# One semaphore for each step of a recurrence, attention with a row to a token, and an up projection parted by columns, in a four-layer conditioned stack on one core

## The chip, the cores and the metric

The kernel runs on one core of a Trainium2 chip. The metric is the device time of one execution in microseconds (us), smaller is better. Three executions of the kernel before took 1957.75, 1958.13 and 1960.11 us; their median is 1958.13.

## What is computed

The input x has 2 sequences of 1024 tokens of width 256, the condition one vector of 256 for each sequence. Four layers follow, each added to x, all in float32:

```python
x = x + L0(x, cond)   # 16 heads over two keys: a learned one and one from cond
x = x + L1(x, cond)   # shared SwiGLU expert (512) + top-2 of 8 gelu experts (128), sum / 3
x = x + L2(cond, x)   # gelu(cond @ Wp + bp) @ Wu + x @ We
x = x + L3(x, cond)   # the recurrence:
#   z = x_t @ Wx + b + h @ Wh;  i, f, o = sigmoid of three quarters, g = tanh of the fourth
#   c = f * c + i * g;  h = o * tanh(c);  the output is h of each of the 1024 tokens
```

Layers 0 to 2 work on each token alone. Layer 3 is serial: step t needs the h of step t-1, 1024 steps in all, for two sequences side by side.

## The kernel before, in words

**One loop, 8 steps to a batch.** The tokens are taken in 128 batches of U = 8 steps (NB = 16 rows: 8 steps by 2 sequences). Each engine has its own loop over the batches; TensorE, ScalarE and VectorE unroll the 8 steps, u = 0 to 7. Layers 0 to 2 of the coming batches are parted into fillers that are placed between the pieces of the recurrence. READY = 16 is the value at which the loops' semaphores start.

**A step of the recurrence.** TensorE waits on `hid`, one semaphore that VectorE raises by 1 at each step; the value it waits for is made by `pe.snap(t + (u + 1))` in every step. Then come `recur_row` for f and for i (L943: 8 products each, h as the weights of a 32 column group of the array, 64 columns moving) and `recur_column` for g and o (L953: 16 products each, 2 columns moving). A float32 product is two weight loads and two matmul records here, so L943 shows 32 of each kind in a step and L953 64. VectorE transposes f and i (L744, L746), ScalarE takes tanh of f (L526), of i and g (L529), of o (L532) and of the cell (L535); VectorE multiplies (L753), forms the cell by a scan (L756), and `close` (L703) writes the new h into `h_ring` and raises `hid`. GpSimd reads h_ring once in a batch, behind the same semaphore.

**TensorE's fillers** stand behind L953 of each step, in program order:

- u = 0: `stream_mm` (L829, 4 products of 128 columns) and `down_mm(0)` (L836, 4 of 256)
- u = 1: `scores` (L793) and `route` (L805, L807) for the next batch, into PSUM bank 5
- u = 2: `down_mm(1)`
- u = 3: `down_mm(2)`, then `attend` (L798): 4 products, value_w as weights of 64 columns, `w1_own` (16 columns) moving; its output `attn_b` has the channels on the partitions. It waits for `mask` of VectorE (L583). All other fillers but the last two products of `route` use column groups of 32
- u = 4: `sum_mm` (L843) and `up_mm` (L815) for K half 1 of the shared expert, 4 products of 256 columns
- u = 5: `up_mm` for K half 0 of all units, 4 products of 512 columns
- u = 6: `inject` (L855), 8 products of 256 columns
- u = 7: `up_mm` for K half 1 of the routed experts, 4 products of 256 columns

The up projection has its sums in `units`, PSUM bank 5, 512 columns: shared expert 0 to 255, the two routed experts of each group 256 to 383 and 384 to 511.

**VectorE's own extras.** At u = 1, behind `close`, `attended` (L599) adds attn_b (PSUM) and x_a (SBUF) into x1, the weights of the next products; it waits for `stream_made` of u = 0. Transposes of the hidden units (L612) are at u = 1, 2 and 7, layer 3's input (L615) and the bias copy (L622) at u = 5; nothing stands at the head of u = 6. VectorE runs in program order, so what stands between `close` and L744 can delay L744.

**ScalarE's extras.** Router and score tanh (L479, L541) at u = 1, `take_partial` (L496) at u = 3, which waits until `attend` is done, the shared tanh (L483) at u = 5 and the gelu (L487) at u = 7.

**GpSimd** runs some 30 small operations for the top-2 gates of a batch, in one chain from L392 to L382, waiting for three reciprocals of VectorE; then `weigh` (L444, which also needs the gelu), the output of the batch (L464, L469) and `move` (L449, a copy of x3 from SBUF to SBUF).

**Before the loop** the weights are loaded and folded and two batches go through layers 0 to 2, with the same helpers; `attend` runs twice there, `attended` twice.

Of the kernel before, what the change touches and what calls it, by code (L numbers as in the profile page):

```python
# [6 lines left out]
ALU = mybir.AluOpType  # L7
# [4 lines left out]
P = 128  # L12
B, T, D = 2, 1024, 256
C = D // P
# [9 lines left out]
U = 8  # L24
# [38 lines left out]
def cond_stack_kernel(nc, x, small, wkv, wq, wproj, up, we, down, wproj2, wu, wx, wh, bias_z, y):  # L63
    ctx = ExitStack()
    with ctx:
# [66 lines left out]
        w1 = sb("w1", [B * HEADS, NB])  # L132
        w1_own = sb("w1_own", [P, NB])
        x1 = sb("x1", [P, C, J, 32])
# [77 lines left out]
        x3_b = bank[7][:, D:D + C * NB].rearrange("p (c t) -> p c t", c=C)  # L212
        attn_b = bank[7][:, D + C * NB:D + 2 * C * NB].rearrange("p (c t) -> p c t", c=C)

        scores_first_b = bank[6][0:B * HEADS, 64:64 + LEAD * NB]
        attn_first_b = bank[6][:, 128:128 + 2 * C * NB].rearrange("p (c n t) -> p c n t", c=C, n=2)
        route_t_b = bank[7][0:B, 448:448 + E]
# [36 lines left out]
        own_out = sem("own_out")  # L254
        attn_made = sem("attn_made")
        x1_out = sem("x1_out")
        route_made = sem("route_made")
# [44 lines left out]
        cell_tanh = sem("cell_tanh")  # L302
        hid = sem("hid")
        h_read = sem("h_read")
# [46 lines left out]
        def _(pool):  # L351
            pool.sem_inc(y_stored, 16)
            for s in (f_made, i_made, o_made, f_turned, a_f, cell, cell_tanh, hid, x_turned, i_based):
                pool.sem_inc(s, READY)
# [104 lines left out]
            with pool.Fori(0, BATCHES) as i:  # L459
                gates(i * U + (READY + U), fall[:, :])  # L460
                weigh(i * U + (READY + U)).then_inc(hid_e_out, U)

                pool.wait_ge(hid, i * U + (READY + U + 1))
                pool.tensor_tensor(half_h[:].rearrange("p c (u b) -> p u c b", b=B), h_ring[:, :, :, WIN - B:WIN],  # L464
                                   half[:, :].unsqueeze(2).unsqueeze(3).to_broadcast([P, U, C, B]),
                                   ALU.mult).then_inc(h_read, U)
                pool.wait_ge(h_read, i * U + (READY + 2 * U))
                pool.wait_ge(y_stored, i * 16 + 16)
                pool.tensor_tensor(y_sb[:, :, :], x3[:, :, 0:NB], half_h[:, :, :], ALU.add).then_inc(y_made, U)  # L469
                pool.wait_ge(y_made, i * U + U)  # L470
                move().then_inc(moved, U)
# [77 lines left out]
        def _(dve):  # L549
# [32 lines left out]
            def mask(src, done, up_to):  # L582
                nc.vector.scalar_tensor_tensor(out=w1_own[0:B * HEADS, :], in0=src, scalar=1.0, in1=own,  # L583
                                               op0=ALU.add, op1=ALU.mult).then_inc(done, up_to)
# [13 lines left out]
            def attended(dst, attn, src):  # L598
                nc.vector.tensor_tensor(dst[:, :, :, 0:NB], attn.unsqueeze(2).to_broadcast([P, C, J, NB]),  # L599
                                        src.unsqueeze(2).to_broadcast([P, C, J, NB]), ALU.add).then_inc(x1_out, U)  # L600

            def hidden_a(count):
# [42 lines left out]
            dve.wait_ge(attn_made, 1)  # L645
            attended(x1_first, attn_first_b[:, :, 0, :], x_first[:, 0, :, :])
            attended(x1, attn_first_b[:, :, 1, :], x_first[:, 1, :, :])
            invert_ratio(U)
# [48 lines left out]
            dve.wait_ge(x_injected, READY)  # L697
            base_f(READY + U)
            dve.wait_ge(terms_set, 5)

            def close(slot):

                nc.vector.scalar_tensor_tensor(out=h_ring[:, slot, :, WIN - B:WIN],  # L703
                                               in0=o_act[:, :].rearrange("p (c b) -> p c b", b=B), scalar=1.0,
                                               in1=c_tanh.rearrange("p (c b) -> p c b", b=B),
                                               op0=ALU.add, op1=ALU.mult).then_inc(hid, 1)


            with dve.Fori(READY, READY + T, U) as t:
                now = t  # L710
                for u in range(U):
# [11 lines left out]
                    elif u == 1:  # L723
                        dve.wait_ge(x_ready, now)
                        dve.wait_ge(stream_made, now)
                        attended(x1, attn_b, x_a[:, :, :])
                    elif u == 2:
                        turn(2, hid_e[:, P:2 * P], hid_e1t, U)
                    elif u == 3:
                        dve.wait_ge(w1_out, now)  # L730
                        mask(w1[:, :], own_out, U)
                    elif u == 4:
                        invert_s(now)
                    elif u == 5:
                        dve.wait_ge(x3_made, now)
                        dve.wait_ge(moved, now)
                        layer3(U)
                    elif u == 7:
                        hidden_s(now)
                        invert_inv(now)  # L740
                        dve.wait_ge(hid_s_out, now)
                        turn(0, hid_s[:, :], hid_st, U)
# [27 lines left out]
        def _(pe):  # L770
# [20 lines left out]
            def scores():  # L791
                for c in range(C):
                    nc.tensor.matmul(scores_b, score_w[:, c, :], x_s[:, c, :], start=(c == 0), stop=(c == C - 1))  # L793

            def attend(attn, weights):
                for c in range(C):
                    for j in range(0, P, 64):
                        last = nc.tensor.matmul(attn[j:j + 64, c], value_w[:, c * P + j:c * P + j + 64], weights,  # L798
                                                start=True, stop=True, skip_group_check=True)
                return last  # L800
# [9 lines left out]

            SHARED, EXPERTS, ALL = slice(0, 2 * P), slice(2 * P, 4 * P), slice(0, 4 * P)

            def up_mm(c, which, first, src):
# [65 lines left out]
            pe.wait_ge(own_first, 1)  # L879
            attend(attn_first_b, own_both[:, :].rearrange("p (n t) -> p n t", n=2)).then_inc(attn_made, 1)  # L880
            pe.wait_ge(value_out, 3)
# [54 lines left out]
            pe.wait_ge(own_first, 2)  # L936
            attend(attn_b, w1_own[:, :])
            pe.wait_ge(wh_scaled, 2)
# [19 lines left out]

            with nc.Fori(READY, READY + T, U, engines=(PE_ENGINE,), head_slot={PE_ENGINE: 0}) as t:
                for u in range(U):  # L960
                    prev = (u - 1) % U
                    now = pe.snap(t + (u + 1))

                    pe.wait_ge(hid, now)
                    recur_row(z_f, GF, u * B, prev).then_inc(f_made, 1)
# [18 lines left out]
                    elif u == 2:  # L984
                        pe.wait_ge(hid_e0t, now)
                        down_mm(1)
                    elif u == 3:
                        pe.wait_ge(hid_e1t, now)
# [4 lines left out]
                    elif u == 4:  # L993
                        pe.wait_ge(partial_out, now)
                        sum_mm().then_inc(x3_made, U)
                        up_mm(1, SHARED, True, x1)
                    elif u == 5:

                        up_mm(0, ALL, False, x1).then_inc(up_made, U)
                    elif u == 6:  # L1000
# [100 lines left out]
```

## Time and profile before

| what | value |
|---|---|
| median of three executions | 1958.13 us |
| the profiled execution | 1957.56 us |
| its span, first to last instruction | 1955.8 us |
| granted TensorE clock, mean | 0.996 |

The profile counts an engine as busy from the start to the modelled end of each instruction; matmuls are pipelined, so busy intervals of TensorE run over one another and reach past the time at which the array can take the next product. PE is the matmul record, PEld the weight load. A row of the timeline gives start, length, engine, line and operation, and in brackets how long the engine was idle before it and what released it. A row with xN merges N records: its length is that of the whole group. The other 1.8 us (1957.56 less 1955.8) lie outside the span.

### The profile page before, as it was taken

The numbers are of one execution on the slowest core, as the hardware profiler recorded it, in microseconds if no ns is written. First come the engines' busy times: TensorE is split into PE (matmuls) and PEld (weight loads), VectorE is DVE, ScalarE is ACT, GpSimd is POOL, SyncE is SP. The second block draws the span as 40 slices with busy tenths as digits, with TensorE's granted clock in tenths as the row PEclk, the third lists the DMA queues.
The fourth block names the chain that finished last, engine by engine and source line by source line (L and its number), as shares of the span: only waits on it lengthen the run. The fifth ranks groups of instructions, "written<-read, shape, count | busy, mean of one in ns | idle before, by whom it ended". The sixth has DMA issues, their size and how long they took to land.

```text
span 1955.8 us, 256304 instructions
## 1 busy us (share of the span) xinstructions
PE 1889.5 (97%) x113680; PEld 1439.8 (74%) x113680; DVE 1390.7 (71%) x7217; ACT 827.2 (42%) x4757; POOL 1133.8 (58%) x4950
## 2 busy tenths in 40 slices
PE   7999999999999999999999999999999999999998
PEld 5777777777777777777777777777777777777776
DVE  2677777777777777777777777777777777777776
ACT  1344444444444444444444444444444444444444
POOL 4555655655555565565555556555555655665565
PEclk9899999999999999999999999999999999999999
DMA  4000000000000000000000000000000000000000
GB/s 170 4 4 3 3 4 3 3 3 4 3 3 4 3 3 3 4 3 3 4 3 3 4 3 3 3 4 3 3 4 3 3 3 4 3 3 4 3 3 3
DMA packets 57724, 14.67 MB, mean 8 GB/s; under 512 B 56176, under 2 KB 56304, under 8 KB 57200
## 3 DMA queue, kind: packets, MB, share of 16 engines
q1 hardware_dynamic: 57712, 14.50, 3.2%
q8 instruction: 9, 0.15, 0.0%
q14 instruction: 3, 0.02, 0.0%
HBM read 12.37 MB, written 2.10 MB: 7 GB/s over the span
## 4 chain that ended last, share of the span: by engine, by line
PE 87%; ACT 6%; DVE 4%; issue 2%; DMA 0%; POOL 0%; DVEq 0%; SPq 0%; POOLq 0%; ACTq 0%
PE psum L953 29%; PE psum L943 29%; PE psum L815 10%; PE psum L836 7%; PE psum L855 6%; DVE h_ring L703 3%; ACT o_act L532 3%; ACT psum L535 2%; PE psum L798 2%; PE psum L829 2%; PE psum L843 1%; PE psum L892 1%; PE psum L793 0%; DMA wkv_sb<-in_wkv 0%; PE psum L776 0%
## 5 line engine op out<-in xcount | busy, mean ns | idle before, releaser
L943 PEld LDWEIGHTS psum<-wh_sb,h_ring 128*2 128x2 f32 (+1 forms) x32768 | 488.4, 90 | 416.6 <-DVE h_ring L703 409.8
L953 PE MATMUL psum<-h_ring,wh_sb 128*32 128x2 f32 x65536 | 765.7, 173 | 1.8 <-issue 1.8
L953 PEld LDWEIGHTS psum<-h_ring,wh_sb 128*32 128x32 f32 x65536 | 725.8, 109 | 2.0 <-issue 2.0
L943 PE MATMUL psum<-wh_sb,h_ring 128*2 128x64 f32 (+1 forms) x32768 | 656.8, 220 | 50.8 <-DVE h_ring L703 20.2
L526 ACT ACTIVATE f_act<-psum 128x4 f32<-128x4 f32 x1024 | 177.3, 173 | 698.6 <-DVE psum L744 698.6
L744 DVE STREAM_TRANSPOSE psum<-psum 128x64 f32<-128x64 f32 x1024 | 266.1, 260 | 274.6 <-PE psum L943 262.7
L815 PE MATMUL psum<-up_sb,x 128*32 128x256 f32 (+1 forms) x3096 | 311.8, 460 | 0.0
L746 DVE STREAM_TRANSPOSE psum<-psum 128x64 f32<-128x64 f32 x1024 | 271.5, 265 | 1.9 <-PE psum L943 1.9
L703 DVE SCALAR_TENSOR_TENSOR h_ring<-o_act,psum 128x4 f32<-128x4 f32 x1025 | 163.0, 159 | 141.9 <-ACT psum L535 115.9
L836 PE MATMUL psum<-down_e,hid_t 128*16 128x256 f32 x3096 | 251.6, 382 | 0.6 <-ACT down_e L507 0.6
L756 DVE TENSOR_TENSOR_SCAN psum<-addend,psum 128x16 f32<-128x16 f32 x1024 | 199.3, 195 | 52.2 <-ACT psum L529 2.4
L532 ACT ACTIVATE o_act<-psum 128x4 f32<-128x4 f32 x1024 | 177.3, 173 | 128.5 <-PE psum L953 2.1
L529 ACT ACTIVATE psum<-psum 128x8 f32<-128x8 f32 x1024 | 165.9, 162 | 54.7 <-PE psum L953 2.6
L753 DVE SCALAR_TENSOR_TENSOR addend<-f_act,psum 128x4 f32<-128x4 f32 x1024 | 165.9, 162 | 14.3
L535 ACT ACTIVATE psum<-psum 128x4 f32<-128x4 f32 x1024 | 161.8, 158 | 0.0
L392 POOL TENSOR_TENSOR num<-one,fall 128x8 f32<-128x8 f32 x128 | 25.6, 200 | 228.6 <-ACT fall L479 228.6
L855 PE MATMUL psum<-wx_sb,x 128*16 128x256 f32 x2064 | 140.0, 381 | 0.4 <-issue 0.4
L398 POOL TENSOR_TENSOR num<-num 128x8 f32<-128x8 f32 x520 | 103.5, 199 | 40.8
L395 POOL TENSOR_TENSOR num<-num,ratio 128x8 f32<-128x8 f32 x130 | 27.1, 208 | 121.0 <-DVE ratio L588 121.0
L444 POOL TENSOR_TENSOR hid_e<-gelu_act,gate_w 128x256 f32<-128x256 f32 x130 | 79.7, 613 | 26.4 <-ACT gelu_act L487 26.1
L798 PEld LDWEIGHTS psum<-w_own,value_w 128*64 128x64 f32 x1032 | 40.7, 137 | 55.2 <-issue 55.2
L496 ACT ACTIVATE partial<-psum 128x256 f32<-128x256 f32 x129 | 49.6, 384 | 71.1 <-PE psum L798 69.8
(142 smaller groups left out, 2286.0 us busy)
## 6 DMA issues: line engine op xcount, KB each, us to landing
x_a<-in_x SPq DMA_DIRECT2D x129, 16.0 KB, 1.6
x_s<-in_x SPq DMA_DIRECT2D x129, 16.0 KB, 1.6
up_sb<-in_up SPq DMA_DIRECT2D x1, 2048.0 KB, 12.7
out_y<-y_sb SPq DMA_DIRECT2D x128, 16.0 KB, 1.4
down_sb<-in_down SPq DMA_DIRECT2D x1, 1536.0 KB, 8.3
wx_sb<-in_wx SPq DMA_DIRECT2D x1, 1024.0 KB, 14.5
wh_sb<-in_wh SPq DMA_DIRECT2D x1, 1024.0 KB, 16.6
wkv_sb<-in_wkv SPq DMA_DIRECT2D x1, 512.0 KB, 4.4
```

The source lines that it names most:

```text
L526: nc.scalar.activation(f_act[:, :].rearrange("p (c b) -> p c b", b=B), by_row(t_f)[:, :, step], ACT.Tanh).then_inc(a_f, 1)
L532: nc.scalar.activation(o_act[:, :].rearrange("p (c b) -> p c b", b=B), by_row(z_o)[:, :, step], ACT.Tanh)
L535: nc.scalar.activation(c_tanh, cell_c, ACT.Tanh).then_inc(cell_tanh, 1)
L703: nc.vector.scalar_tensor_tensor(out=h_ring[:, slot, :, WIN - B:WIN], in0=o_act[:, :].rearrange("p (c b) -> p c b", b=B), scalar=1.0, in1= ...
L744: nc.vector.transpose(t_f, z_f).then_inc(f_turned, 1)
L746: nc.vector.transpose(t_i, z_i).then_inc(i_and_c_in, 1)
L756: nc.vector.tensor_tensor_scan(cell_all, addend[:, :], factor, 0.0, ALU.add, ALU.mult).then_inc(cell, 1)
L815: last = nc.tensor.matmul(units[32 * j:32 * (j + 1), which], src[:, c, 0, :], up_sb[:, c, j, which], start=first, stop=not first, skip_gro ...
L836: last = nc.tensor.matmul(partial_b[32 * k:32 * k + NB, :], hid_t[:, blk * 32:blk * 32 + NB], down_e[:, blk, :], start=False, stop=False, ...
L855: last = nc.tensor.matmul(z_x[32 * j:32 * j + NB, :, :], x3[:, c, NB:2 * NB], wx_v[:, c, :, j, :], start=False, stop=(c == C - 1), skip_gr ...
L943: last = nc.tensor.matmul(z[32 * j:32 * j + row + B, :], h_ring[:, prev, c, WIN - B - row:WIN], wh_v[:, c, g, j, :], start=False, stop=(c ...
L953: last = nc.tensor.matmul(by_row(z)[32 * j:32 * (j + 1), m, row:row + B], wh_v[:, c, g, j, 32 * m:32 * (m + 1)], h_ring[:, prev, c, WIN - ...
```

## The change

All steps: `hid` becomes a list of 8 semaphores, one for each u, each raised by U = 8 once in a batch; TensorE forms its register `now` once in a batch, not once in a step. `close(slot)` raises `hid[(slot + 1) % U]`.

Attention: `w1_own` becomes 32 columns wide and is the weight operand; 4 products with 64 moving columns of value_w write a row to a token, 32 rows to each of the four groups of partitions. VectorE transposes the 128x64 result in blocks of 32 into `attn_t` in SBUF, at the head of u = 6, behind a wait on `x1_out`; `attended` at u = 1 reads `attn_t`, behind a wait on `attn_turned`. The same goes for the two batches before the loop, whose two attentions become one call of 4 products, one transpose and two `attended`; one more transpose stands ahead of VectorE's loop.

Up projection: the columns of the second routed expert (384 to 511) of K half 0 move from u = 5 to u = 2, behind `down_mm(1)` and a wait on `w1_out`; u = 5 keeps 384 columns.

```diff
-        w1_own = sb("w1_own", [P, NB])
+        w1_own = sb("w1_own", [P, 32])
+        attn_t = sb("attn_t", [P, C, 32])
+        attn_first_t = sb("attn_first_t", [P, C, 32])
...
-        attn_b = bank[7][:, D + C * NB:D + 2 * C * NB].rearrange("p (c t) -> p c t", c=C)
+        attn_b = bank[7][:, D + C * NB:D + C * NB + HC]
...
-        attn_first_b = bank[6][:, 128:128 + 2 * C * NB].rearrange("p (c n t) -> p c n t", c=C, n=2)
+        attn_first_b = bank[6][:, 128:128 + HC]
...
-        hid = sem("hid")
+        hid = [sem(f"hid_{u}") for u in range(U)]
...
-                pool.wait_ge(hid, i * U + (READY + U + 1))
+                pool.wait_ge(hid[0], i * U + (READY + 2 * U))
...
+            def turn_attention(up_to):
+                nc.vector.transpose(attn_t[:, :, :].rearrange("p c t -> p (c t)"), attn_b).then_inc(attn_turned, up_to)
...
-            attended(x1_first, attn_first_b[:, :, 0, :], x_first[:, 0, :, :])
-            attended(x1, attn_first_b[:, :, 1, :], x_first[:, 1, :, :])
+            nc.vector.transpose(attn_first_t[:, :, :].rearrange("p c t -> p (c t)"),
+                                attn_first_b).then_inc(attn_turned, U)
+            dve.wait_ge(attn_turned, U)
+            attended(x1_first, attn_first_t[:, :, 0:NB], x_first[:, 0, :, :])
+            attended(x1, attn_first_t[:, :, NB:2 * NB], x_first[:, 1, :, :])
...
             base_f(READY + U)
+            dve.wait_ge(attn_made, 2)
+            turn_attention(READY)
             dve.wait_ge(terms_set, 5)
...
-                                               op0=ALU.add, op1=ALU.mult).then_inc(hid, 1)
+                                               op0=ALU.add, op1=ALU.mult).then_inc(hid[(slot + 1) % U], U)
...
                         dve.wait_ge(stream_made, now)
-                        attended(x1, attn_b, x_a[:, :, :])
+                        dve.wait_ge(attn_turned, now)
+                        attended(x1, attn_t[:, :, 0:NB], x_a[:, :, :])
...
+                    elif u == 6:
+                        dve.wait_ge(x1_out, now)
+                        turn_attention(U)
...
+            value_v = value_w[:, :].rearrange("p (c j m) -> p c j m", c=C, j=J)
+
             def attend(attn, weights):
-                for c in range(C):
-                    for j in range(0, P, 64):
-                        last = nc.tensor.matmul(attn[j:j + 64, c], value_w[:, c * P + j:c * P + j + 64], weights,
-                                                start=True, stop=True, skip_group_check=True)
+                for j in range(J):
+                    last = nc.tensor.matmul(attn[32 * j:32 * (j + 1), :], weights, value_v[:, :, j, :],
+                                            start=True, stop=True, skip_group_check=True)
                 return last
...
+            BUT_EXPERT_1, EXPERT_1 = slice(0, 3 * P), slice(3 * P, 4 * P)
...
+                now = pe.snap(t + U)
                 for u in range(U):
                     prev = (u - 1) % U
-                    now = pe.snap(t + (u + 1))
-                    pe.wait_ge(hid, now)
+                    pe.wait_ge(hid[u], now)
...
                     elif u == 2:
                         pe.wait_ge(hid_e0t, now)
                         down_mm(1)
+                        pe.wait_ge(w1_out, now)
+                        up_mm(0, EXPERT_1, True, x1)
...
                         sum_mm().then_inc(x3_made, U)
-                        up_mm(1, SHARED, True, x1)
+                        up_mm(1, SHARED, False, x1)
                     elif u == 5:
-                        up_mm(0, ALL, False, x1).then_inc(up_made, U)
+                        up_mm(0, BUT_EXPERT_1, False, x1).then_inc(up_made, U)
```

## Rows read from the trace of the kernel before

**Rows 1.** The page, part 1, then two groups of its part 5 (busy us, mean ns | idle before, releaser)

```profile
PE 1889.5 (97%) x113680; PEld 1439.8 (74%) x113680; DVE 1390.7 (71%) x7217; ACT 827.2 (42%) x4757; POOL 1133.8 (58%) x4950
...
L943 PEld LDWEIGHTS psum<-wh_sb,h_ring 128*2 128x2 f32 (+1 forms) x32768 | 488.4, 90 | 416.6 <-DVE h_ring L703 409.8
...
L798 PEld LDWEIGHTS psum<-w_own,value_w 128*64 128x64 f32 x1032 | 40.7, 137 | 55.2 <-issue 55.2
```

**Rows 2.** The timeline, `close` (L703) on VectorE at ten places: start us, us

```profile
41.92 0.16 DVE L703 SCALAR_TENSOR_TENSOR h_ring<-o_act,psum 128x4 f32<-128x4 f32 x1
...
65.74 0.16 DVE L703 SCALAR_TENSOR_TENSOR h_ring<-o_act,psum 128x4 f32<-128x4 f32 x1 [0.22 <-ACT psum L535]
...
1001.36 0.16 DVE L703 SCALAR_TENSOR_TENSOR h_ring<-o_act,psum 128x4 f32<-128x4 f32 x1 [0.22 <-ACT psum L535]
...
1003.18 0.16 DVE L703 SCALAR_TENSOR_TENSOR h_ring<-o_act,psum 128x4 f32<-128x4 f32 x1 [0.22 <-ACT psum L535]
...
1008.65 0.16 DVE L703 SCALAR_TENSOR_TENSOR h_ring<-o_act,psum 128x4 f32<-128x4 f32 x1 [0.22 <-ACT psum L535]
...
1010.60 0.16 DVE L703 SCALAR_TENSOR_TENSOR h_ring<-o_act,psum 128x4 f32<-128x4 f32 x1 [0.22 <-ACT psum L535]
...
1012.43 0.16 DVE L703 SCALAR_TENSOR_TENSOR h_ring<-o_act,psum 128x4 f32<-128x4 f32 x1
...
1014.32 0.16 DVE L703 SCALAR_TENSOR_TENSOR h_ring<-o_act,psum 128x4 f32<-128x4 f32 x1
...
1016.21 0.16 DVE L703 SCALAR_TENSOR_TENSOR h_ring<-o_act,psum 128x4 f32<-128x4 f32 x1 [0.22 <-ACT psum L535]
...
1951.76 0.16 DVE L703 SCALAR_TENSOR_TENSOR h_ring<-o_act,psum 128x4 f32<-128x4 f32 x1 [0.22 <-ACT psum L535]
```

**Rows 3.** The timeline, step u = 1 of one batch

```profile
1003.39 0.45 PEld L943 LDWEIGHTS psum<-wh_sb,h_ring 128*4 128x4 f32 x32 [0.43 <-DVE h_ring L703]
...
1003.87 0.27 DVE L744 STREAM_TRANSPOSE psum<-psum 128x64 f32<-128x64 f32 x1
...
1005.21 0.45 PEld L943 LDWEIGHTS psum<-wh_sb,h_ring 128*6 128x6 f32 x32 [0.17 <-DVE h_ring L703]
```

**Rows 4.** Stretches: us, busy us (x records) of the five engines, clock, DMA share, GB/s

```profile
50.00:55.00 5.00, 4.34 (x171) 3.38 (x163) 1.56 (x8) 1.13 (x6) 2.33 (x9) 0.50 0.02 3
...
500.00:514.85 14.85, 14.47 (x888) 11.03 (x887) 10.79 (x57) 6.40 (x38) 8.71 (x38) 1.00 0.02 3
```

**Rows 5.** DMA queues from 36 to 66 us: packets, MB, share

```profile
q8 instruction: 8, 0.13, 1.9%
```

**Rows 6.** The timeline, end of step u = 3 of the same batch, TensorE

```profile
1008.07 0.64 PE L836 MATMUL psum<-down_e,hid_t 128*16 128x256 f32 x7
...
1008.64 0.31 PEld L798 LDWEIGHTS psum<-w_own,value_w 128*64 128x64 f32 x8 [0.42 <-issue]
...
1008.98 0.46 PEld L943 LDWEIGHTS psum<-wh_sb,h_ring 128*10 128x10 f32 x32
```

**Rows 7.** The timeline, steps u = 5 and 6 of the same batch, TensorE

```profile
1011.85 1.08 PE L815 MATMUL psum<-up_sb,x 128*32 128x512 f32 x7
...
1012.64 0.55 PEld L943 LDWEIGHTS psum<-wh_sb,h_ring 128*14 128x14 f32 x32 [0.62 <-DVE h_ring L703]
...
1012.71 0.66 PE L943 MATMUL psum<-wh_sb,h_ring 128*14 128x64 f32 x32
```

**Rows 8.** The timeline, before the loop and at its start

```profile
41.51 0.41 PE L798 MATMUL psum<-w_own,value_w 128*64 128x16 f32 x8
```

**Rows 9.** The timeline, step u = 1 of the same batch, GpSimd and VectorE

```profile
1003.50 0.21 POOL L449 COPY x<-x 128x32 f32<-128x32 f32 x1
...
1003.59 0.29 DVE L599 TENSOR_TENSOR x<-psum,x_a 128x128 f32<-128x128 f32 x1 [0.26 <-PE psum L836]
```

**Rows 10.** A line of VectorE with both inputs in SBUF: duration ns min/median/max, first and last start

```profile
L631 DVE TENSOR_TENSOR we_sb<-we_sb,small_sb x2: 270/270/271, 12.8 to 13.0; 128x128 f32<-128x128 f32 x2
```

**Rows 11.** The page, part 5: `weigh` on GpSimd

```profile
L444 POOL TENSOR_TENSOR hid_e<-gelu_act,gate_w 128x256 f32<-128x256 f32 x130 | 79.7, 613 | 26.4 <-ACT gelu_act L487 26.1
```

More of the change, by code:

```diff
@@ L255, in cond_stack_kernel @@
         attn_made = sem("attn_made")
+        attn_turned = sem("attn_turned")
         x1_out = sem("x1_out")
@@ L352, in _ @@
             pool.sem_inc(y_stored, 16)
-            for s in (f_made, i_made, o_made, f_turned, a_f, cell, cell_tanh, hid, x_turned, i_based):
+            for s in (f_made, i_made, o_made, f_turned, a_f, cell, cell_tanh, x_turned, i_based, *hid):
                 pool.sem_inc(s, READY)
@@ L582, in mask @@
             def mask(src, done, up_to):
-                nc.vector.scalar_tensor_tensor(out=w1_own[0:B * HEADS, :], in0=src, scalar=1.0, in1=own,
+                nc.vector.scalar_tensor_tensor(out=w1_own[0:B * HEADS, 0:NB], in0=src, scalar=1.0, in1=own,
                                                op0=ALU.add, op1=ALU.mult).then_inc(done, up_to)
@@ L879, in _ @@
             pe.wait_ge(own_first, 1)
-            attend(attn_first_b, own_both[:, :].rearrange("p (n t) -> p n t", n=2)).then_inc(attn_made, 1)
+            attend(attn_first_b, own_both[:, :]).then_inc(attn_made, 1)
             pe.wait_ge(value_out, 3)
@@ L936, in _ @@
             pe.wait_ge(own_first, 2)
-            attend(attn_b, w1_own[:, :])
+            attend(attn_b, w1_own[:, :]).then_inc(attn_made, 1)
             pe.wait_ge(wh_scaled, 2)
```

## The prediction

> **What bounds the kernel now.** The page comes first, and it misleads: TensorE is busy for 97% of the span [rows 1]. In the same rows its weight loads for the next h (L943) stood idle for 409.8 us until `close` had written h, so TensorE waits for VectorE in most steps. The second view is the timeline, read only for the starts of `close`, which are 1 step apart [rows 2]. One batch takes 1016.21 - 1001.36 = 14.85 us, and all but the first do: (1951.76 - 65.74) / 127 = 14.85. The first takes 65.74 - 41.92 = 23.82. Within the batch the step of u = 0 takes 1.82, those of u = 1, 2 and 3 together 5.47 (1.82 each), u = 4 takes 1.95, u = 5 takes 1.83, and u = 6 and 7 take 1.89 each.
>
> Steps with quite different fillers take the same 1.82 us, so there the serial chain decides. The third view, one such step, shows it [rows 3]: first weight load at 1003.39, transpose of f at 1003.87, the next step's first load at 1005.21, 1.82 later, after TensorE had been idle for 0.17. What the change can win without shortening that chain is what the three long steps have above 1.825: 0.12 at u = 4, 0.065 at u = 6, 0.065 at u = 7, together 0.25 us in a batch, or 32 us over 128. For each of them I ask which filler held TensorE.
>
> *u = 4.* The filler of u = 3 is too long [rows 6]. The eight matmul records of `down_mm(2)` begin at about 1008.06. At the rate worked out below (54 ns for one of 256 columns) the array has taken them by 1008.49, yet the loads of `attend` begin only at 1008.64, and L943 at 1008.98, though h was written at 1008.65 + 0.16 = 1008.81 [rows 2]. From 1008.49 to 1008.98 is 0.49 us for `attend`, with 0.15 empty ahead of it (the trace puts 0.42 us of idle loader time down to "issue", and the page has 55.2 us of that in the whole run, all at this line [rows 1]). It is the only filler here with weights 64 columns wide. I take that the array has to run empty between the two widths, before and after.
>
> *u = 6.* The filler of u = 5 is eight records of 512 columns [rows 7], from 1011.84. The next step's loads start in time, at 1012.64, its matmuls at 1012.71: late by 0.07. So eight records of 512 columns take 12.71 - 11.84 = 0.87 us, 109 ns each, 54 for 256 columns, 27 for 128, 14 for 64.
>
> *u = 7.* `inject` has 16 records of 256 columns, 0.87 us as well, and is not touched.
>
> **The change part by part.**
>
> *Attention in four products.* Four products of 64 columns are eight records, 8 x 14 = 0.11 us, in groups of 32 columns like their neighbours. Then TensorE is through at 1008.49 + 0.11 = 1008.60, 0.21 before h is there, and the step of u = 4 begins with h: it goes from 1.95 to about 1.83. By `close` the gain is 0.12 in a batch. It can't be more, since the chain holds the step then, and the other end is nothing, should the new products wait as long as the old ones. I take 0.12, as the two changes of width are gone. `take_partial` on ScalarE starts earlier by some 0.3 us, which no one waits for.
>
> *The transpose.* VectorE gets one more STREAM_TRANSPOSE of 128x64 at the head of u = 6; its like takes 0.27 [rows 3]. It is put between `close` and L744, a stretch of VectorE from 1003.34 to 1003.87 in a step without extras (0.16 after `close` starts at 1003.18, until f is there [rows 2, 3]), so 0.53 wide. 0.27 fits, with 0.2 or more to spare; price 0. If the cover went, the price would be what reaches past L744. Its wait on `x1_out` is for an operation of VectorE itself, five steps back. `attended` at u = 1 waits on `attn_turned`, three steps old by then; price 0 as well.
>
> *`attended` from SBUF.* Now 0.29 us from PSUM and SBUF, 1003.59 to 1003.88, and L744 starts at 1003.87 [rows 3, 9]: this one has no slack. With both inputs in SBUF an operation of the same size took 0.270 [rows 10]. Price 0, at best 0.02.
>
> *128 columns of the up projection moved.* u = 5 keeps 384 columns: 8 x 82 = 0.66 us, through at 1012.50, ahead of h (1012.43 + 0.16 = 1012.59). So the step of u = 6 loses its 0.065. At u = 2, `down_mm(1)` (0.44) gets 0.22 behind it: 0.66, as much as u = 0 has now with 128 and 256 columns, and the step behind u = 0 is not late: 1003.39 is 0.05 after h (1003.34) [rows 2, 3]. The wait on `w1_out` is for ScalarE's operation behind the step before; u = 0 has a wait between its two fillers too. Behind it in TensorE's queue stands the step of u = 3, so were it late, all would be; I price it at 0. Gain 0.065, bounds 0 and 0.07.
>
> *One semaphore for each step, one register.* The only thing that it removes is TensorE's forming of a register ahead of each wait. In seven steps of eight TensorE idles there anyway, 0.17 us in the fullest of those shown [rows 3]: covered. L943 starts 0.05 after the end of `close` (1003.34 to 1003.39); I can bound a gain by a hop of nothing, 0.05 x 1024 = 51 us, but I see no register in that gap, since it would be formed before h comes. Price 0. Without that cover, it would be one register operation for each step, for which no row has a time.
>
> *Before the loop and its first batch.* The transpose ahead of the first `attended` and the one ahead of the first `close` cost 0.27 each with nothing beside them; `attend` at 41.51, 0.41 long with its last end [rows 8], gives about 0.3 back, but only the second time does VectorE wait near it. Sum +0.5, bounds 0 and +0.7. The first batch takes 8.97 us longer than the others. Instructions come in over their own queue at that time (8 packets, 0.13 MB, from 36 to 66 us [rows 5]) and the granted clock is at 0.50, the 1.2 GHz level, from 50 to 55 us, after TensorE had stood still for want of instructions; later it is at 1.00 [rows 4]. The loop's body has some 1775 records [rows 4] and gets 16 more. How that falls on the packets is not to be read from here: 0, with bounds of -4 and +4.
>
> **The sum.** (0.12 + 0.065) x 127 batches = 23.5 us less, 0.5 more: 1957.56 - 23.0 = 1934.6 for the profiled execution. That execution is 0.57 under the median of three, so against the median it would be 1935.1. I say 1935.
>
> **The rivals.**
>
> *A, the forecast* (0.72): the two long steps become chain-bound. 1935; with the first batch's bounds and 0.03 a batch for a residue or for a little of the 0.02 at `attended`, 1930 to 1941.
>
> *B, half of it* (0.13): one of the two steps stays late. Only the columns: 1958 - 8 = 1950. Only the attention: 1958 - 15 = 1943. For it speaks that the gap ahead of `attend` bears the name "issue" and not that of a width; against it that no other filler shows it.
>
> *C, the chain gets shorter too* (0.06): the register or the value compared lies between h and L943 after all. If it has 0.01 to 0.02 of the 0.05, another 10 to 20 us: 1915 to 1925. Against it: TensorE has been idle for 0.17 to 0.43 us at that point [rows 3].
>
> *D, slower* (0.05): `attended` and GpSimd get into each other's way at u = 1. At present `move` (L449) runs from 1003.50 to 1003.71 and reads SBUF, and `attended` starts at 1003.59 beside it with one input from PSUM [rows 9]. With two inputs from SBUF it may have to wait until L449 is done. L744 follows at once, so each ns of it is in the step. The price is up to 1003.71 - 1003.59 + 0.1 = 0.22 us a batch, 28 us: 1963. It decides from 0.18 us on, where it eats up the 23 us; at 0.1 it leaves 1948. Against it: GpSimd gains only some 0.1 us in the batch that gets shorter by 0.185, since `weigh` waits for the gelu now (26.1 us in 128 batches, 0.20 each [rows 11]) and then for its own gates; so L449 would start about 0.08 later against `attended`, and VectorE may well be first. The Trainium skill, "SBUF — State Buffer", section "Who interferes with whom", states the rule: a VectorE instruction with two SBUF inputs contends with a GpSimd instruction that reads SBUF, and whoever issues first has the port for the whole instruction. No row here shows VectorE with two SBUF inputs beside a busy GpSimd for long enough to tell. By that rule the result depends on who is first.
>
> *E, it doesn't do what it says* (0.04): some wait is late in a way that I don't see, or both steps keep their length: 1957 to 1960.
>
> **How the numbers follow.** About 0.2% (4 us) can be told from no change. Faster by more: A, B and C, 0.72 + 0.13 + 0.06 = 0.91. Within: E, 0.04. Slower: D at more than the 0.18, 0.05. The range is A's own 1930 to 1941, carried up to 1948, so that it takes in the columns failing (1943) and a D at half price. C, D, E and the upper half of B are left out, about 0.2.
>
> **What would show it.** Right: `close` to `close` is 1.82 or 1.83 in all steps but u = 7 (1.89); a batch takes 14.665; no "issue" idle at the line of `attend`; L943's loads follow h by 0.05 at u = 4. The matmuls of u = 6 start with their loads. Wrong: a step of u = 1 above 1.82 with `attended` starting later than 0.25 after `close` has ended is D; all steps below 1.82 is C; an idle loader ahead of `attend` or of the columns at u = 2 is B; a first batch far from 23.8 is the start's bounds.

## The result and the profile after

The changed kernel takes 2007.75 us (median of four, 2006.75 to 2008.01) against 1958.28 for the kernel before; the ratio is 1.025 with a 95% interval of 1.0232 to 1.0268. It is slower by 49 us where the forecast said faster by 23. The profiled execution has 2007.65 us, its span 2005.7, its mean granted clock 0.997 (0.996 before).

From the page of the changed kernel: part 1, the instruction queue, then two groups of part 5 (the loads for the next h, and `close`). The second block is the group of `close` in the kernel before, L703:

```profile
PE 1906.6 (95%) x114704; PEld 1466.1 (73%) x114704; DVE 1436.8 (72%) x7347; ACT 832.3 (41%) x4757; POOL 1141.9 (57%) x4950
...
q8 instruction: 9, 0.15, 0.0%
...
L963 PEld LDWEIGHTS psum<-wh_sb,h_ring 128*2 128x2 f32 (+1 forms) x32768 | 467.8, 90 | 460.6 <-DVE h_ring L716 458.4
...
L716 DVE SCALAR_TENSOR_TENSOR h_ring<-o_act,psum 128x4 f32<-128x4 f32 x1025 | 163.1, 159 | 204.0 <-ACT psum L540 177.0
```

```profile
L703 DVE SCALAR_TENSOR_TENSOR h_ring<-o_act,psum 128x4 f32<-128x4 f32 x1025 | 163.0, 159 | 141.9 <-ACT psum L535 115.9
```

TensorE waits more for h (458.4 us at L963, 409.8 before [rows 1]), and VectorE waits more, in `close`, for ScalarE's tanh of the cell: 177.0 against 115.9 us. Each `close` is as long as before, 159 ns. The chain of the step has become longer, between those two instructions. Lines of one step (u = 3 of one batch) and the start of the next, changed kernel:

```profile
1002.38 0.45 PEld L963 LDWEIGHTS psum<-wh_sb,h_ring 128*8 128x8 f32 x32 [0.28 <-DVE h_ring L716]
...
1002.86 0.27 DVE L761 STREAM_TRANSPOSE psum<-psum 128x64 f32<-128x64 f32 x1 [0.31 <-PE psum L963]
...
1003.58 0.20 DVE L773 TENSOR_TENSOR_SCAN psum<-addend,psum 128x16 f32<-128x16 f32 x1
1003.63 0.38 PEld L817 LDWEIGHTS psum<-value_w,w_own 128*32 128x32 f32 x8
...
1003.81 0.16 ACT L540 ACTIVATE psum<-psum 128x4 f32<-128x4 f32 x1
1003.84 0.32 PE L817 MATMUL psum<-value_w,w_own 128*32 128x64 f32 x8
1004.07 0.16 DVE L716 SCALAR_TENSOR_TENSOR h_ring<-o_act,psum 128x4 f32<-128x4 f32 x1 [0.29 <-ACT psum L540]
...
1004.28 0.46 PEld L963 LDWEIGHTS psum<-wh_sb,h_ring 128*10 128x10 f32 x32 [0.28 <-DVE h_ring L716]
```

The same places in the kernel before:

```profile
1004.58 0.20 DVE L756 TENSOR_TENSOR_SCAN psum<-addend,psum 128x16 f32<-128x16 f32 x1
...
1004.81 0.16 ACT L535 ACTIVATE psum<-psum 128x4 f32<-128x4 f32 x1
1005.00 0.16 DVE L703 SCALAR_TENSOR_TENSOR h_ring<-o_act,psum 128x4 f32<-128x4 f32 x1
```

A step is 1004.28 - 1002.38 = 1.90 long, not 1.82. Load to transpose is 0.48 as in [rows 3], scan to tanh 0.23 in both, `close` to the next load 0.21 in both. From the start of the tanh to that of `close` it is 0.26 here and 0.19 before: 0.07 more, and no other part of the step has changed by more than 0.01. `attend` is where it was forecast: its loads start at 1003.63 with no idle time, and L963 at 1004.28 had waited 0.28 for h.

By the starts of `close`, medians over the 128 batches, in us:

| step u | 0 | 1 | 2 | 3 | 4 | 5 | 6 | 7 | batch | first batch |
|---|---|---|---|---|---|---|---|---|---|---|
| before | 1.82 | 1.82 | 1.83 | 1.83 | 1.94 | 1.83 | 1.89 | 1.88 | 14.85 | 23.82 |
| forecast | 1.82 | 1.82 | 1.83 | 1.83 | 1.83 | 1.83 | 1.83 | 1.89 | 14.67 | 23.8 |
| changed | 1.88 | 1.89 | 1.90 | 1.90 | 1.90 | 1.90 | 1.90 | 1.96 | 15.23 | 25.14 |

The changed kernel is the forecast plus 0.07 in every step: 8 x 0.07 = 0.56 a batch, 71 us over 127 batches, with the 23.5 us of gain inside.

### The profile page after: what moved, and what is told of

Read it like the earlier page. It is cut to its first block, busy times and chain, and to the rows that moved or that the text cites. A ratio compares the mean times of both kernels' runs of the same rounds, so it can differ in the third digit from the quotient of the medians.

```text
span 2005.7 us, 258620 instructions
## 1 busy us (share of the span) xinstructions
PE 1906.6 (95%) x114704; PEld 1466.1 (73%) x114704; DVE 1436.8 (72%) x7347; ACT 832.3 (41%) x4757; POOL 1141.9 (57%) x4950
## 2 busy tenths in 40 slices
DMA packets 57724, 14.67 MB, mean 7 GB/s; under 512 B 56176, under 2 KB 56304, under 8 KB 57200
## 4 chain that ended last, share of the span: by engine, by line
PE 82%; ACT 8%; DVE 5%; issue 4%; DVEq 1%; POOL 0%; DMA 0%; SPq 0%; POOLq 0%; ACTq 0%
PE psum L963 30%; PE psum L973 29%; PE psum L835 7%; PE psum L856 6%; PE psum L875 6%; ACT o_act L537 4%; DVE h_ring L716 4%; ACT psum L540 4%; PE psum L849 2%; PE psum L912 1%; DVEq L725 1%; PE psum L863 0%; PE psum L810 0%; DMA wkv_sb<-in_wkv 0%; PE psum L793 0%
## 5 line engine op out<-in xcount | busy, mean ns | idle before, releaser
L963 PEld LDWEIGHTS psum<-wh_sb,h_ring 128*2 128x2 f32 (+1 forms) x32768 | 467.8, 90 | 460.6 <-DVE h_ring L716 458.4
L963 PE MATMUL psum<-wh_sb,h_ring 128*2 128x64 f32 (+1 forms) x32768 | 652.8, 220 | 81.4 <-DVE h_ring L716 34.8
L835 PE MATMUL psum<-up_sb,x 128*32 128x256 f32 (+3 forms) x4120 | 340.1, 387 | 0.0
L716 DVE SCALAR_TENSOR_TENSOR h_ring<-o_act,psum 128x4 f32<-128x4 f32 x1025 | 163.1, 159 | 204.0 <-ACT psum L540 177.0
L770 DVE SCALAR_TENSOR_TENSOR addend<-f_act,psum 128x4 f32<-128x4 f32 x1024 | 166.1, 162 | 14.8
L397 POOL TENSOR_TENSOR num<-one,fall 128x8 f32<-128x8 f32 x128 | 25.8, 201 | 249.1 <-ACT fall L484 249.1
L835 PEld LDWEIGHTS psum<-up_sb,x 128*32 128x32 f32 x4120 | 114.0, 108 | 17.1 <-issue 0.9
L407 POOL TENSOR_TENSOR sel<-s_all,small_sb 128x8 f32<-128x8 f32 x130 | 26.3, 202 | 107.2 <-DVE s_all L597 107.2
```

The lines of the kernel that those rows point to most:

```text
L835: last = nc.tensor.matmul(units[32 * j:32 * (j + 1), which], src[:, c, 0, :], up_sb[:, c, j, which], start=first, stop=not first, skip_gro ...
L963: last = nc.tensor.matmul(z[32 * j:32 * j + row + B, :], h_ring[:, prev, c, WIN - B - row:WIN], wh_v[:, c, g, j, :], start=False, stop=(c ...
```

## The experiments

**Round one: each part alone.** The 0.07 sits ahead of an instruction whose operands didn't change. Of the diff only its `then_inc` touches it, but an extra transpose, an extra semaphore and a missing register instruction on TensorE came at the same time. So the parts first. Semaphores alone:

```diff
+        hid = [sem(f"hid_{u}") for u in range(U)]
+                                               op0=ALU.add, op1=ALU.mult).then_inc(hid[(slot + 1) % U], U)
+                now = pe.snap(t + U)
+                    pe.wait_ge(hid[u], now)
```

> The semaphore for each step and the one register in a batch, alone, on the kernel before. In the changed kernel each step has 0.07 us more between the tanh of the cell on ScalarE and close on VectorE. Theory S (the semaphore part causes it): 8 x 0.07 = 0.57 us a batch on top of 14.85, so 15.42 and about 2031 us. Theory X (the attention part causes it, by its extra transpose, its extra semaphore or its wider operand): 14.85 a batch, 1958 us.

Measured: 2009.35 us, ratio 1.0264 (1.0247 to 1.0281). A batch takes 15.27; the steps 1.88 to 1.90, with 1.94 at u = 4 and 1.96 at u = 7. So theory S, though 2031 was too much. At u = 4 and u = 6 the fillers of the kernel before are late anyway, by 0.12 and 0.065, and cover it, which leaves 0.42 a batch. The scan, tanh and `close` of one step of this run:

```profile
1002.47 0.19 DVE L756 TENSOR_TENSOR_SCAN psum<-addend,psum 128x16 f32<-128x16 f32 x1
...
1002.70 0.16 ACT L535 ACTIVATE psum<-psum 128x4 f32<-128x4 f32 x1
1002.96 0.16 DVE L703 SCALAR_TENSOR_TENSOR h_ring<-o_act,psum 128x4 f32<-128x4 f32 x1 [0.21 <-ACT psum L535]
```

0.26 again. The run also tells what makes the step of u = 7 long, which the prediction had laid to `inject` on TensorE. If TensorE came late there, the later h would be covered, as it is at u = 4 and u = 6; but the step grows by the whole 0.07, to 1.96. The load and the matmul of L943 now start together, 0.21 after `close`, and the transpose L744 still comes 0.81 after it, not 0.70 as in the step before, since three extras of VectorE stand ahead of it (L609, L596, L612):

```profile
1010.61 0.16 DVE L703 SCALAR_TENSOR_TENSOR h_ring<-o_act,psum 128x4 f32<-128x4 f32 x1
...
1010.82 0.48 PEld L943 LDWEIGHTS psum<-wh_sb,h_ring 128*16 128x16 f32 x32 [0.29 <-DVE h_ring L703]
1010.82 0.65 PE L943 MATMUL psum<-wh_sb,h_ring 128*16 128x64 f32 x32
...
1011.18 0.31 DVE L612 STREAM_TRANSPOSE hid_t<-hid_s 128x128 f32<-128x128 f32 x1
1011.42 0.22 DVE L744 STREAM_TRANSPOSE psum<-psum 128x64 f32<-128x64 f32 x1
```

The attention alone (all of the diff's edits to `attend`, `w1_own`, `attn_t`, `attended`, and nothing else):

> The attention part alone, on the kernel before. Theory S: only the gain of 0.12 at u = 4, 14.73 a batch, about 1943 us. Theory X: that gain and 0.57 on top, 15.30 a batch, about 2016 us.

Measured: 1942.61 us, ratio 0.9927 (0.9910 to 0.9943), 14.74 a batch, with 1.83 at u = 4 and all else as before. Theory S, within a microsecond. What it shows at u = 3 and 4:

```profile
1000.47 0.38 PEld L814 LDWEIGHTS psum<-value_w,w_own 128*32 128x32 f32 x8
...
1000.68 0.33 PE L814 MATMUL psum<-value_w,w_own 128*32 128x64 f32 x8
1000.84 0.16 DVE L714 SCALAR_TENSOR_TENSOR h_ring<-o_act,psum 128x4 f32<-128x4 f32 x1 [0.22 <-ACT psum L538]
...
1001.05 0.46 PEld L959 LDWEIGHTS psum<-wh_sb,h_ring 128*10 128x10 f32 x32 [0.20 <-DVE h_ring L714]
```

TensorE's loader had been idle for 0.20 when h came; in the kernel before, L943 started 0.17 after h was there [rows 6].

The same run shows `attended` (here L602) with both inputs in SBUF beside GpSimd's copy (here L452), the meeting that rival D was about:

```profile
1010.47 0.21 POOL L452 COPY x<-x 128x32 f32<-128x32 f32 x1
...
1010.58 0.29 DVE L602 TENSOR_TENSOR x<-attn_t,x_a 128x128 f32<-128x128 f32 x1 [0.32 <-PE psum L852]
...
1010.79 0.26 DVE L759 STREAM_TRANSPOSE psum<-psum 128x64 f32<-128x64 f32 x1
```

They run side by side in 127 of the 128 batches, and `attended` takes 0.293 in the median, against 0.291 from PSUM. In the one batch in which it also ran beside `weigh` it took 0.437, and 0.41 to 0.44 in the same batch of each of the other three traces with this edit; in the kernel before it took 0.291 beside `weigh`. So there is such a cost, but the copy brings on next to none of it.

The columns alone:

```diff
                         down_mm(1)
+                        pe.wait_ge(w1_out, now)
+                        up_mm(0, EXPERT_1, True, x1)
...
+                        up_mm(1, SHARED, False, x1)
...
+                        up_mm(0, BUT_EXPERT_1, False, x1).then_inc(up_made, U)
```

> The 128 columns of the up projection moved, alone, on the kernel before. Both theories: 0.065 less at u = 6, 14.785 a batch, about 1950 us. If this part were the cause of the 0.07 in each step (theory Y): 15.36, about 2023 us.

Measured: 2230.37 us (2206 to 2258 in four runs), ratio 1.131 (1.1262 to 1.1359). No theory had that. The median batch is 14.79, the step of u = 6 takes 1.83: the gain is there to the letter. But 18 of the 128 batches take 30.3 us. The attention and the columns, without the semaphore part:

> Attention and columns, with the one semaphore and the register of each step as before. Theory S: the forecast of the record without its semaphore part, 14.665 a batch, 1935 us. Theories X and Y: 15.23 a batch, 2008 us.

Measured: 2283.16 us, ratio 1.1641 (1.1593 to 1.1689). Median batch 14.68, just as forecast, and 22 batches of about 30 us. The instruction queues of the two runs (packets, MB; columns alone, then both parts):

```profile
q8 instruction: 171, 2.80, 0.6%
```

```profile
q8 instruction: 207, 3.39, 0.7%
```

Nine packets had been enough for the kernel before, and eight of them came from 36 to 66 us, before and in its first batch [rows 5]. 171 is 9 and 18 times 9, 207 is 9 and 22 times 9: one more fetch of the whole loop for each long batch (in both traces the nine packets fall inside the long batches), 2.80 MB / 171 = 16.4 KB a packet. The head of such a batch in the run with both parts, and then three stretches of 15 us, the first of them inside that batch (us, busy us (x records) of PE, PEld, DVE, ACT, POOL, clock, DMA share, GB/s):

```profile
174.92 0.76 PEld L960 LDWEIGHTS psum<-wh_sb,h_ring 128*2 128x2 f32 x32 [4.99 <-issue]
```

```profile
180.00:195.00 15.00, 13.15 (x475) 10.15 (x471) 5.39 (x28) 3.09 (x21) 6.26 (x28) 0.50 0.03 6
195.00:210.00 15.00, 14.67 (x786) 11.51 (x774) 9.46 (x49) 5.61 (x33) 5.38 (x23) 0.83 0.03 4
210.00:225.00 15.00, 14.72 (x918) 11.56 (x918) 11.16 (x59) 6.40 (x37) 8.96 (x39) 1.00 0.02 3
```

At the head of the batch TensorE's loader stands still for 4.99 us with nothing that it waits for ("issue") while the packets come in, and the granted clock falls to 0.50 (1.2 GHz), at which it stays for 17 to 27 of the 30 us of these batches: half as many matmuls in the stretch. Both together cost 30.3 - 14.8 = 15.5 us; the runs don't part them. That is 18 x 15.5 = 279 of the 287 us by which its span of 2237.1 is above 1950.

Why has the changed kernel no such batches, with the same columns? Counting the instructions of one pass of TensorE's loop in the program (a float32 product is four; the records of the traces give the same counts): 1782 before, 1798 with the columns alone or with attention and columns, 1791 in the whole change, since the one register for a batch takes seven register instructions out. That makes theory K of the next round.

**Round two: which part of the semaphore part, and is it length.** Three kernels separate the raise by 8, the number of semaphores and the missing register instruction. The whole change with a raise by 1 (1792 instructions):

```diff
-                                               op0=ALU.add, op1=ALU.mult).then_inc(hid[(slot + 1) % U], U)
+                                               op0=ALU.add, op1=ALU.mult).then_inc(hid[(slot + 1) % U], 1)
-            with nc.Fori(READY, READY + T, U, engines=(PE_ENGINE,), head_slot={PE_ENGINE: 0}) as t:
-                now = pe.snap(t + U)
+            with nc.Fori(3, 3 + BATCHES, 1, engines=(PE_ENGINE,), head_slot={PE_ENGINE: 0}) as t:
+                now = pe.snap(t * U)
-                    pe.wait_ge(hid[u], now)
+                    pe.wait_ge(hid[u], t)
-                pool.wait_ge(hid[0], i * U + (READY + 2 * U))
+                pool.wait_ge(hid[0], i + 4)
```

(the eight start at 2, not at READY.)

> The whole change, but close raises each of the eight semaphores by 1, not by 8; TensorE's loop counts batches from 3, waits on hid[u] with the loop's own register and makes the value for its other waits as 8 times it. Theory S1 (the raise by 8 is what costs 0.07 in each step): close again follows the tanh of the cell by 0.03 us, a batch takes 14.67 and the run 1935 us. Theories S2 (eight semaphores in place of one) and S3 (no register instruction ahead of TensorE's wait): 15.23, 2008 us. If the loop's body, one instruction longer than the changed kernel's, no longer fits where instructions are kept, there are many more instruction packets than 9 and 2200 us or more, but the step in the batches without a fetch tells the same.

Measured: 1937.28 us, ratio 0.9891 (0.9875 to 0.9908). 9 packets, steps 1.82 to 1.83 and 1.88 at u = 7, a batch 14.67 or 14.68, first batch 25.81. **It beats both kernels.** The place where the changed kernel lost (L965 of u = 4, then `close` and L965 of u = 5):

```profile
1000.00 0.46 PEld L965 LDWEIGHTS psum<-wh_sb,h_ring 128*10 128x10 f32 x32 [0.21 <-DVE h_ring L718]
...
1001.62 0.16 DVE L718 SCALAR_TENSOR_TENSOR h_ring<-o_act,psum 128x4 f32<-128x4 f32 x1 [0.23 <-ACT psum L542]
1001.83 0.46 PEld L965 LDWEIGHTS psum<-wh_sb,h_ring 128*12 128x12 f32 x32 [0.49 <-DVE h_ring L718]
```

1.83 from load to load. The kernel before with its one semaphore raised by 8 (`.then_inc(hid, U)`, waits for 8 times the value):

> The kernel before with its one semaphore, but close raises it by 8 and TensorE and GpSimd wait for 8 times the value. S1: as with the semaphore part alone, 15.27 a batch, 2009 us. S2 and S3: 14.85, 1958 us.

Measured: 2012.56 us, ratio 1.0276 (1.0259 to 1.0293), 15.28 a batch. Eight semaphores raised by 8, with TensorE's register instruction in each step (`pe.wait_ge(hid[u], pe.snap(t + U))`):

> The kernel before with eight semaphores raised by 8, and TensorE's register instruction kept in each step. S1 and S2: 15.27 a batch, 2009 us. S3: 14.85, 1958 us.

Measured: 2012.31 us, ratio 1.0274 (1.0257 to 1.0292), 15.28 a batch. Only S1 foretold all three: the raise by 8 costs the 0.07, with one semaphore or eight, with the register instruction or without. The length of the loop, tried by itself on the kernel before, with no other work:

```diff
+                for k in range(16):
+                    pe.sem_inc(h_pad, 1)
                 for u in range(U):
```

> The kernel before with 16 more raises of an unused semaphore at the head of TensorE's loop, no other work: as many more instructions as the columns part has. Theory K (the loop's body of TensorE no longer fits where instructions are kept, and is fetched again in some batches, which lowers the clock too): q8 has over 100 instruction packets, not 9, some batches take 30 us, and the run 2200 us or more. Theory L (the moved columns cost it by what they do, the 16 instructions are harmless): 9 packets, 14.85 to 15.1 a batch, 1958 to 1990 us.

Measured: 2960.3 us; 1798 instructions, 31 batches of 30.8 us behind the first, and

```profile
q8 instruction: 289, 4.73, 0.8%
```

So the fetches come back with no column moved, as theory K has it. But 2960 is not their price alone. Even the shortest batches are long (16.98 us), so the raises cost something by themselves, and the median of all batches is 20.06, with the granted clock at 0.50 for 3 to 22 us of many that have no fetch.

**Round three.** Does the price grow with the value, what is left of the pad when the loop is short enough, and do the other engines pay? The raise by 2 is the kernel with one semaphore and 2 in place of 8:

> The kernel before with its one semaphore raised by 2 at each step, and waits for twice the value. Theory S1a (any raise by more than 1 costs the whole): 15.27 a batch, 2010 us, as with 8. Theory S1b (the cost grows with the value, 0.07 for 8, so 0.01 for 2): 14.93 a batch, 1968 us.

Measured: 2012.05 us, ratio 1.0275 (1.0258 to 1.0292), 15.28 a batch: S1a. It is a step from 1 to 2, not a slope.

> As the run with 16 added raises of an unused semaphore at the head of TensorE's loop, with 8 of them: the body is then as long as the changed kernel's, which keeps to 9 packets. Theory K (length decides the fetches): 9 packets, the added raises show in the step of u = 0 alone, 1.2 us at the most (half of the 2.4 or so with 16), so 1958 to 2110 us. Theory L (the raises themselves bring on the fetches): about half as many packets as with 16, over 100.

Measured: 2070.86 us, ratio 1.0574 (1.0556 to 1.0592); 1790 instructions and

```profile
q8 instruction: 9, 0.15, 0.0%
```

Theory K. All of it is in the step of u = 0, 2.70 for 1.82; the other seven steps are those of the kernel before. In the records seven of the raises are instructions of their own, 0.15 us apart (the eighth stands on the loop's register instruction); part of their time falls where TensorE was idle, so the step grows by 0.88. Eight raises more, in the run before, add another 16.98 - 15.73 = 1.25, 0.16 each. The kernels with 9 packets have loops of 1775 to 1792 instructions, the three with more have 1798, so the limit of this loop on TensorE lies between these two. 1792 is seven times 256, and the packets are 16.4 KB. The Trainium skill, "Runtime: NRT & Kernel Launch", section "Instruction fetch mechanics", says that TensorE keeps 2048 instructions, filled in blocks of 256; the block agrees with the runs as far as they go, but a loop of 1798 was already fetched again here, 250 short of that size.

Then ScalarE: the tanh of the cell raises `cell_tanh` by 8, VectorE waits for 8 times the value.

```diff
-                    nc.scalar.activation(c_tanh, cell_c, ACT.Tanh).then_inc(cell_tanh, 1)
+                    nc.scalar.activation(c_tanh, cell_c, ACT.Tanh).then_inc(cell_tanh, U)
```

> The kernel before, with ScalarE raising cell_tanh (the tanh of the cell, in the chain of every step) by 8, not by 1, and VectorE waiting for 8 times the value. If a raise by 8 costs on ScalarE what it costs on VectorE: 15.27 a batch, about 2010 us. If it is VectorE's alone: 14.85, 1958 us.

Measured: 2002.82 us, ratio 1.0230 (1.0213 to 1.0247), 15.19 a batch, so nearer to the first forecast. ScalarE pays too, some 0.06 a step, and again ahead of the instruction that has the raise:

```profile
1001.72 0.20 DVE L757 TENSOR_TENSOR_SCAN psum<-addend,psum 128x16 f32<-128x16 f32 x1
...
1002.01 0.16 ACT L536 ACTIVATE psum<-psum 128x4 f32<-128x4 f32 x1
...
1002.20 0.16 DVE L704 SCALAR_TENSOR_TENSOR h_ring<-o_act,psum 128x4 f32<-128x4 f32 x1 [0.28 <-ACT psum L536]
```

The tanh starts 0.29 behind the scan, not 0.23, and `close` follows after 0.19 as it did before. The cost has moved to where the raise is.

> The kernel before, with TensorE raising f_made (in the chain of every step, at the eighth product of L943) by 8, not by 1. If a raise by 8 costs on TensorE too, ahead of the instruction that bears it: up to 0.07 a step, 15.27 a batch, 2010 us. If it doesn't: 1958 us.

Measured: 1957.96 us, ratio 1.000 (0.999 to 1.001), 14.85 a batch. This raise costs nothing.

**What stands ahead of `close`.** The traces also have a record for each instruction that only waits or raises, which the page doesn't count as busy. In the kernel before, `close` carries its wait on `cell_tanh` and its raise in one instruction. In the four runs on the kernel before with `close` raising by 2 or by 8 VectorE has 897 more such records (2454, not 1557): one in seven steps of eight, and one behind the loop. Each holds the wait on `cell_tanh`, starts 0.195 after the start of the tanh, where `close` itself started before (0.190), and `close` starts 0.066 after it. In the eighth step a wait instruction stood there already and took this wait in; there the gap grows by 0.057, which is why u = 0 has 1.88. The changed kernel has the same 897 and 258 for the waits of the attention part; with the raise by 1 only the 258 are left. ScalarE's run has 1024 more, each 0.062 ahead of its tanh.

In none of the fourteen traces does an instruction that works on data carry both a wait and a raise by more than 1; with a raise by 1 VectorE alone has 5136 that carry both in the kernel before. So the 0.07 is the price of one more instruction in the chain: the wait, which the larger raise has driven out of `close`. And the last run doesn't show that TensorE is exempt. The matmul that raises `f_made` carries no wait (TensorE's waits stand on its weight loads), no record was added (14 on TensorE in both), and there was nothing to drive out.

## Why the prediction was wrong, point by point

- *What bounds the kernel*: right where it counts: the serial chain decides in the short steps, so a cost on it comes back in nearly every one of the 1024. Of the three long steps it read two rightly. The third, u = 7, it laid to `inject`, and there VectorE's extras ahead of L744 decide (see the run with the semaphores alone); as neither was touched, the sum didn't suffer. The prediction had that sentence and then priced the one edit to the chain's last instruction at 0.
- *Attention in four products*, -0.12 a batch: right (-0.11 measured alone, 15.0 us). The gap ahead of `attend` went with the 64 wide weights; that their width made it wasn't tested by itself, as the operands changed roles in the same edit.
- *The transpose* and *`attended` from SBUF*, 0: right. The step of u = 6 loses its 0.065 as forecast in the kernel with the raise by 1, and the step of u = 1 is 1.82 in the run with the attention alone. Rival D, the quarrel with GpSimd's copy, cost nothing in the step: `attended` took 0.293 beside it in the run with the attention alone and 0.304 with the raise by 1, not 0.291. It also started 0.07 later than before (0.48 behind `close`, not 0.41), with one more wait ahead of it, and L759 still came at 0.69. So the "no slack" of the prediction was wrong: the transpose starts while `attended` is still in its last 0.08.
- *128 columns moved*, -0.065: right as to the array (14.79 alone), and wrong as to its instructions. "The loop's body has some 1775 records [rows 4] and gets 16 more" was priced at 0 with the first batch alone in view. By itself this edit costs 273 us; in the change it costs nothing, only because the semaphore part takes seven instructions out.
- *One semaphore for each step, one register*, 0: **this is the step that failed.** "The only thing that it removes is TensorE's forming of a register" left out what it adds: `close` raises by 8, not by 1, and with that its wait on the tanh became an instruction of its own. That is 0.07 ahead of each `close`, 0.56 a batch with the other gains made, 71 us. The bounds looked at the hop from `close` to TensorE, and only for a gain; the cost came on the other side of `close`, from ScalarE.
- *Before the loop and its first batch*: +0.5 and 0 with -4 and +4. The first `close` came 0.1 and 0.2 later in the changed kernel and in the one with the raise by 1, and their first batch went from 23.8 to 25.1 and 25.8, +1.3 and +2.0 (one profiled execution each). That is inside the bounds. It is one half of why the work of the forecast takes 1937.3 and not 1935; the other is that a batch got shorter by 0.175, not by 0.185, 1.3 us over 127.
- *Rivals*: none was it. The slower rival had one mechanism at u = 1, and the steps of the changed kernel are longer by the same 0.07 everywhere. (The upper end of A adds up to 1935 + 4 + 0.03 x 127 = 1943, not 1941; the range took that in.)

The sum with the measured terms: 1957.56 - 22.2 (127 batches, the kernel with the raise by 1 against the kernel before) + 70.7 (127 batches, the changed kernel against it) + 1.3 (first batch) + 0.1 (before it) = 2007.5, and the profiled execution took 2007.65.

Open: why a wait and a raise by more than 1 don't stand in one instruction, and what an instruction of TensorE with both would pay. How long the loop may be exactly, between 1792 and 1798, wasn't tried, nor why only some passes of a loop over that length are fetched.

## What to carry to other kernels

Price what an edit does to the `then_inc` of an instruction in the serial chain as well as to its waits. Where such an instruction of VectorE or ScalarE also waits, raise by 1, and put the multiple into the waiting side's register; a larger raise belongs on an instruction that has no wait of its own or that nothing waits for closely. In a long unrolled loop count TensorE's instructions before adding work to an idle place; sixteen too many cost more than ten such gains, and an edit that looks idle may be what makes the room. Undo the parts of a change one by one: here the sum hid two gains, one loss and one dependence.

## What the runs showed of the hardware that was not expected

- An instruction on VectorE that waits, and raises a semaphore by 2 or 8, has its wait in an instruction of its own 0.066 us ahead, and starts 0.07 us later than the same with 1 (0.26 against 0.19 behind its releaser); on ScalarE 0.06. A raise by 8 on a matmul, which carries no wait here, cost nothing (ratio 1.000).
- TensorE's loop of 1792 instructions or fewer was fetched once (9 packets of 16.4 KB in the whole run); of 1798, 18 to 31 passes in 128 were fetched again. In the two runs without added raises such a pass cost some 15.5 us, with the clock at 0.50 for 17 to 27 us of it.
- Semaphore raises that stand by themselves in TensorE's stream follow one another by 0.15 us.
- VectorE's `attended` with both inputs in SBUF took 0.41 to 0.44 us beside GpSimd's `weigh` (one batch in each of four traces) and 0.293 beside its short copy (0.304 in two of the four), against 0.291 with one input in PSUM.
